# Row maxima placed by VectorE's load: one in diagonal pairs of steps, up to three in the others, 14 to 26 steps ahead of their scores

## What is computed

```python
latent_kv = x @ w_kv_down
kv = latent_kv @ w_kv_up
k, v = (kv[..., :HD], kv[..., HD:])
q = (x @ w_q).reshape(Bx, Tx, N_HEAD, HEAD_SIZE)
att = jnp.einsum('bqhd,bkhd->bhqk', q, k) * scale
att = jnp.where(causal, att, -jnp.inf)
att = jax.nn.softmax(att, axis=-1)
y = jnp.einsum('bhqk,bkhd->bqhd', att, v)
y = y.reshape(Bx, Tx, HD)
return y @ w_out
```

## Time and profile before

| | us |
|---|---|
| median of 3 runs | 2247.56 |
| lowest, highest | 2245.97, 2248.89 |
| the profiled execution | 2246.04 |
| its span, first to last instruction | 2244.7 |
| of it the attention steps | 330 to 2147 |

### The profile page before, as it was taken

One profiled execution on the slowest core, in us unless ns is written; L12 is line 12 of the kernel. 1 busy time (PEld: TensorE's weight loads), 2 busy tenths in 40 slices (PEclk: granted clock), 3 DMA queues, 4 the chain that ended last, 5 costly groups with the idle time before them and its releaser, 6 DMA issues.

```text
span 2244.7 us, 35674 instructions
## 1 busy us (share of the span) xinstructions
PE 2060.4 (92%) x13104; PEld 1269.9 (57%) x13104; DVE 1331.9 (59%) x2713; ACT 1102.8 (49%) x2226; POOL 1426.5 (64%) x812
## 2 busy tenths in 40 slices
PE   5998669999999999999989999999999999999989
PEld 3666345555555555555555555555555555555556
DVE  5888446575656565656565656566656565656353
ACT  4775534444444444444454444444444444444575
POOL 0333305776777777777757677777777777777832
PEclk9999769999999999999999999999999999999999
DMA  3000000000000000000000000000000000000001
GB/s 108 1 1 1 10 7 6 10 18 10 18 11 18 11 18 11 18 11 18 10 18 11 13 11 19 9 22 6 19 9 23 11 18 11 18 11 11 25 24 57
DMA packets 25788, 37.03 MB, mean 16 GB/s; under 512 B 6544, under 2 KB 14864, under 8 KB 25616
## 3 DMA queue, kind: packets, MB, share of 16 engines
q1 hardware_dynamic: 25616, 34.76, 5.0%
HBM read 30.02 MB, written 4.46 MB: 15 GB/s over the span
## 4 chain that ended last, share of the span: by engine, by line
PE 65%; DVE 19%; ACT 6%; issue 5%; POOL 4%; DMA 0%; ACTq 0%; DVEq 0%; POOLq 0%
PE heads_out L796 18%; PE beside L615 14%; PE two_heads L755 8%; PE scores L778 4%; PE scores L784 4%; PE scores L782 4%; PE scores L780 4%; DVE part_max L985 4%; PE scores L615 2%; POOL acc L1276 2%; ACT prob L1194 2%; DVE stats L835 2%; PE beside L807 2%; PE beside L763 1%; PE two_heads L615 1%
## 5 line engine op out<-in xcount | busy, mean ns | idle before, releaser
L1276 POOL TENSOR_TENSOR acc<-acc,prob 128x1024 f32<-128x1024 f32 (+3 forms) x512 | 1017.1, 1987 | 228.5 <-ACT prob L1194 172.7
L1194 ACT ACTIVATE prob<-scores 128x512 f32<-128x512 f32 (+3 forms) x1280 | 579.4, 538 | 636.4 <-DVE scores L995 327.8
L985 DVE TENSOR_REDUCE part_max<-two_heads 128x2 f32<-128x1024 f32 x384 | 468.7, 1221 | 309.1 <-PE two_heads L755 308.8
L796 PE MATMUL heads_out<-prob,V 128*64 128x512 f32 (+3 forms) x2560 | 549.1, 550 | 0.0
L755 PE MATMUL two_heads<-k_hi,q_hi 64*128 64x512 f32 (+3 forms) x1280 | 278.9, 431 | 70.2 <-DVE part_max L982 36.5
L982 DVE CUSTOM_DVE_ANT_0 two_heads<-two_heads,mask 128x128 f32<-128x128 f32 (+3 forms) x512 | 241.8, 514 | 119.2 <-PE two_heads L755 119.1
L796 PEld LDWEIGHTS heads_out<-prob,V 128*64 128x64 f32 x2560 | 157.8, 138 | 232.1 <-issue 210.4
L755 PEld LDWEIGHTS two_heads<-k_hi,q_hi 64*128 64x128 f32 x1280 | 121.3, 186 | 239.3 <-issue 102.4
L778 PE MATMUL scores<-q_hi,k_hi 64*128 64x512 f32 (+3 forms) x1280 | 236.9, 364 | 1.0 <-ACT neg_max L1181 0.8
L784 PE MATMUL scores<-neg_max,sel 64*128 64x512 f32 (+3 forms) x1280 | 236.9, 363 | 0.0
L782 PE MATMUL scores<-q_lo,k_hi 64*128 64x512 f32 (+3 forms) x1280 | 236.3, 363 | 0.0
(11 more groups left out here) (298 smaller groups left out, 3011.4 us busy)
## 6 DMA issues: line engine op xcount, KB each, us to landing
rden<-rden_rows SPq DMA_DIRECT2D x128, 128.0 KB, 2.9
wP_raw<-wPair SPq DMA_DIRECT2D x16, 384.0 KB, 3.2
X<-u SPq DMA_DIRECT2D x8, 512.0 KB, 8.7
out<-X SPq DMA_DIRECT2D x8, 512.0 KB, 2.9
den<-den_rows SPq DMA_DIRECT2D x64, 4.0 KB
rden_rows<-inverse SPq DMA_DIRECT2D x64, 4.0 KB, 1.4
wA_sb<-wA SPq DMA_DIRECT2D x1, 768.0 KB, 6.8
wFa<-wF SPq DMA_DIRECT2D x1, 768.0 KB, 7.7
```

Source lines behind the costliest of these rows:

```text
L796: made = pe.matmul(heads_out[head(h), x0:], V[(idx - j + c) % NVS][:, tt, head(h)], prob[step % NPROB][:, h, x0:], start=t == 0, stop=t == ...
L985: made = ve.reduce_max(part_max[:, t, :, c:c + 1], two_heads[:, :, 0:width], AX.X)
L1194: ac.activation(prob[step % NPROB][:, h, x0:], bank(task, h)[:, x0:], ACT.Exp).then_inc(empty(task, h)[0], 1)
L1276: po.tensor_tensor(total[:, :, x0:], total[:, :, x0:], new[:, :, x0:], ALU.add).then_inc(acc_ok, 1)
```

## The change

The lead stays 20 in the middle, but may swing by 6. A pair of steps is `diagonal` if one of its two steps is. In such a pair one maximum is placed, behind the scores, as long as the maxima are less than 26 steps ahead; in other pairs up to three, under the same limit; below 14 ahead up to three anywhere. The maximum ahead of the scores is left out in diagonal pairs, and wherever the last thing TensorE was given in the pair before is a maximum (`adjacent`); it then comes behind the scores, the filler or the weighings. `filler()` now says whether it placed something. `fillers()` is as before and reads `LEAD`, 20.

```diff
--- before.py
+++ after.py
@@ -29,7 +29,7 @@
 NPROB = 4
 NQ = 4
 NKS, NVS = 7, 6
-LEAD = 20
+LEAD, SWING = 20, 6
 NDEN, QUAD = 8, 32
 DVE_OUT = 62
 MIX = [(1, 0), (1, 1), (0, 0), (0, 1)]
@@ -351,9 +351,11 @@
 
         def filler(latest):
             open_ = sorted((x for x in fillers if x[0] <= s and x[2] not in self.done), key=lambda x: x[1])
-            if open_ and open_[0][1] <= latest:
-                fillers.remove(open_[0])
-                self.need(*open_[0][2])
+            if not open_ or open_[0][1] > latest:
+                return False
+            fillers.remove(open_[0])
+            self.need(*open_[0][2])
+            return True
 
         def output(idx):
 
@@ -379,7 +381,7 @@
         self.need("key", 1)
         self.need("query", 1)
         self.need("turn_max", 0)
-        self.in_steps = True
+        self.in_steps, adjacent = True, False
         for s in range(0, len(steps) + 2, 2):
             for load in sorted(x for x in loads if x[0] <= s):
                 loads.remove(load)
@@ -387,8 +389,10 @@
             for b in [STATS_BEFORE[UNITS[i]] for i in range(NU) if s == self.start[i] and UNITS[i] in STATS_BEFORE]:
                 side += self.mixer_stats(b, 2 if b else 3, NT)
             urgent = max([self.start[i] + TPB * (UNITS[i][2] + 1) for i in range(NU) if self.start[i] <= s + 4])
-            goal = min(len(maxima), max(urgent, min(s + 2 + LEAD, at + 3)))
-            if at < goal:
+            diagonal = any(t >= TPB * UNITS[idx][2] for idx, t in steps[s:s + 2])
+            ahead_of = max(min(s + 2 + LEAD + SWING, at + (1 if diagonal else 3)), min(s + 2 + LEAD - SWING, at + 3))
+            goal = min(len(maxima), max(urgent, ahead_of))
+            if at < goal and not diagonal and not adjacent:
                 maximum()
             due("invert")
             for step in steps[s:s + 2]:
@@ -406,12 +410,13 @@
                 if t == TPB * (UNITS[idx][2] + 1) - 1:
                     self.need("take_out", idx)
                     output(idx)
-            if at < goal:
+            adjacent = at < goal
+            if adjacent:
                 maximum()
             due("two_parts")
             due("scale_out")
-            if not due("denominators"):
-                filler(s + 8)
+            if due("denominators") or filler(s + 8):
+                adjacent = False
             if side:
                 self.add_all(side.pop(0))
             self.add_all(ahead.get(s - len(steps), []))
```

## The result

The changed kernel takes 2400.5 us (median of 4 runs, 2398.2 to 2413.2) against 2248.2 for the kernel before in the same session: 1.069 times as long, interval 1.067 to 1.072. The loss is 152 us where 87 were forecast, and 2400.5 is outside the range of 2280 to 2390.

What follows compares the result with a forecast made beforehand. TensorE was taken as the bound. Query waits of 99 us plus 58 us for maxima close together, less a 70 us gain, made +87 us: 2335 us, own range 2295 to 2375, widened to 2280 to 2390.

Steps and rivals of the forecast that it cites:

- The query's chain: Maxima directly behind their own query matmuls wait for `q_hi`, then `q_lo`: 53 new cases, 99 us lost.
- the price of `wP_lo`: Both halves, 1.06 us each on VectorE, between first and second maximum of three: 12 times 1.84 us, 22 us.
- the closeness: Maxima close to each other without long work between make TensorE wait: 58 us together, bounds 30 to 95.
- the 6 us of `turn_max`: Transposition needing bank 7 while VectorE's X add is behind a masked maximum: 16 times 0.4 us, 6 us.
- the clock: Rival: 5% of the attention steps' time, 91 us, falls to 1.2 GHz, losing 45 us: 2380 us; chance 0.07.
- The gain: Removed waits: 60 us of maxima, mostly behind diagonals' short scores, and 10 us of denominators for `k_lo`; 70 us.
- VectorE's busy time: Sign in the profile after: VectorE's busy time, like ScalarE's and GpSimd's, is the same within 1%.
- TensorE busy 87 to 88% of the steps: Sign in the profile after: TensorE is busy 87 to 88% of a longer stretch of attention steps.
- backlog: Rival: VectorE's work bunches in pairs with three maxima, 0.5 us at some 130 waits: +65, 2400 us; chance 0.09.
- only the queries: Rival: VectorE is always fast enough between maxima, so the 58 us falls away: 2277 us; chance 0.06.
- faster: Rival: the query's wait only replaces waits TensorE has anyway, leaving 58 less 70: 2235 us; chance 0.05.
- diagonals still wait: Rival: the change doesn't do what it says and diagonals still wait: +60, 2395 us; chance 0.03.

Runs made afterwards that it cites:

- e1_hold: Changed kernel, but queries or keys needed by the next eight maxima replace the filler, and no maximum stands directly behind its own query: 2297.9 us, 1.024.
- e2_forced: Kernel before, with queries from unit 3 on no longer fillers, so each is built directly ahead of its first maximum: 2328.3 us, 1.037.
- e5_hold_wlo_gpsimd: Changed kernel with no maximum directly behind its own query and the `wP_lo` subtractions moved from VectorE to GpSimd: 2232.1 us, 0.994.
- e6_spaced: Kernel before, lead 20, maxima behind scores and weighings, the latter left out ahead of a diagonal's end, made up behind a query or value: 2199.3 us, 0.980.
- e4_wlo_one_input: Changed kernel with the two-input `wP_lo` subtraction replaced by a one-input product of `wP_raw` with zero, same place: 2345.5 us (one run).
- e10_wlo_apart: Changed kernel with the two `wP_lo` halves in different pairs again, one ahead of `k_lo`, one behind the next maximum's reduction: 2347.5 us, 1.044.
- e3_wlo_gpsimd: Changed kernel with the `wP_lo` subtractions issued by GpSimd in place of VectorE: 2344.2 us, 1.043.

## Why the prediction was wrong, step by step

**The direction and the main term were right.** The query's chain was put at 1.57, 2.08 and 2.19 us in 26, 14 and 13 cases, 99 us. Its waits came to 82 us of idle time and 7 at `den_rows`. Taking it out gave 103 us (e1_hold); that this is so near 99 is luck, since 18 us of clock are in it, which the term didn't have, and 12 us of new waits work against them. Adding it to the order of before cost 95 us of waits and 82 of time (e2_forced). In the profile after, the case behind a full pair and the one behind the first pair of a diagonal read:

```profile
624.38 0.50 PE L760 MATMUL two_heads<-k_hi,q_hi 64*128 64x512 f32 x2 [1.50 <-DVE q_lo L973]
```

```profile
689.25 0.49 PE L760 MATMUL two_heads<-k_hi,q_hi 64*128 64x512 f32 x2 [1.66 <-DVE q_lo L973]
```

The mask holds the chain up less than I had it (1.66 us idle where 2.08 start to start were put, against 1.50 and 1.57 behind a full pair), and behind denominators the wait is divided: 1.50 for `q_lo` and 0.48 at the query's first matmul for `den_rows`, the 6.6 us of the last row of the waits; 1.98 in all against 2.19.

**The step that failed is the price of `wP_lo`.** I took 1.06 us for each half, the mean of the earlier trace rows, and 22 us for the 12 places. A group's mean is no price when the durations differ by four times: before, they ran from 0.415 to 1.704 us. It was the mean of four free ones and 28 that were held for the rest of one sum each, mostly 0.83 and 1.42. The change puts both halves behind each other into a stretch where GpSimd has 0.17 us between two sums, and so adds a whole sum. The chain from first to third maximum that I wrote as 5.77 us has 4.14 in place of 2.12, which is 2.0 more and 3.4 idle in place of the 1.84. That is 41 us of idle time and 56 to 66 us of time with what it does to the clock, where the sum had 22. It alone carries the closeness, 58 us, to the upper end of its bounds of 30 to 95: with the other waits of that kind in the trace (11.3 us at denominators, where I had 12; 9.5 at projections, where I had 10; 6.7 at keys, where I had 8; 6.8 behind the weighings of a short diagonal, where I had nothing) the idle time is 75 us, 90 to 100 with the price of `wP_lo` in full. The small terms were near. Of the 6 us of `turn_max` the list of waits shows nothing.

**The second failed step is the clock: the sum had nothing for it, and the rival with a chance of 0.07 came true.** I had 45 us if 91 us of the steps fell to 1.2 GHz; 90 us more did, worth some 40. Counted by kind and not by place, it is the larger half of the 65 us that the forecast lacked. My reason against it, that the waits are single ones among dense matmuls, is right as a picture and wrong as an argument: one wait of 3.4 us was followed by 3 to 4 us at 1.2 GHz. The Trainium skill's rule ("TensorE: Matmul & The Clock Gate", Part 1), that the clock is throttled unless TensorE's activity releases it, pointed this way, and I gave it too little. The total agrees with it (97 us more idle time, 90 us more at 1.2 GHz), e2_forced does not (89 us more idle time, 19 us less at 1.2 GHz). Part of this is in the amounts above and must not be added to them. The split by time, from the pairs of runs that differ in one thing, is

| | us | from |
|---|---|---|
| query waits | +103 | changed less e1_hold |
| `wP_lo`, with the query waits gone | +66 | e1_hold less e5_hold_wlo_gpsimd |
| all the rest of the change | -15 | e5_hold_wlo_gpsimd less before in its session (2247.5) |
| sum | +154 | measured 152 in the first session |

**The gain was overrated.** The waits behind short scores did go: behind the scores of 128 columns one of 0.6 us is left of 61 with 43.8 us. But the rest of the change, in which they stand as -70 and the other closeness as +36, was to give -34 us and gave -15. The 12 us of new waits that e1_hold itself makes are in this figure; without them it would be about -27, and the query waits about +115. One reason may be that idle time ahead of a matmul isn't all time that can be had back, though no run shows that for this order: e6_spaced has 2.9 us less of it in 40 steps than before (1.0 against 3.9) and is 1.8 us shorter (108.1 against 109.9). I had counted each at its idle time plus 0.1. The other way it doesn't hold: the changed kernel's 121.7 us are 11.8 more than 109.9, with 8.6 us more idle time and 3.4 us of low clock.

**VectorE's busy time** was to stay within 1%; it rose by 49 us, 3.7%. That line of the test pointed at the cause, since nothing was added to VectorE: the 32 instructions of `wP_lo` last 24 us longer in all (58.2 against 33.9). The rest is no work: all 2713 durations together grew by only 26 us, so the records overlap less. The sign "TensorE busy 87 to 88% of the steps" was no test: by my own sum it would be 1724 of 1904 us, 91%, and 1782.6 of 1973 is 90%. The other rivals, backlog, "only the queries", faster and "diagonals still wait", are out: the waits have their few places, and e5_hold_wlo_gpsimd is 168 us under the changed kernel. The backlog's 2400 us is the measured number by chance: it wanted 0.5 us in each of some 130 waits, and the price sits in 12 waits of 3.4 us and in the clock.

**Which wait brings the clock down?** In the changed order both kinds do. From 330 us to the end of the steps its trace has 33 stretches at 1.2 GHz. Nineteen of them, 82 us, begin within 4 us of the start of a query wait, of which there are 53; eleven, 38 us, within 5 us of the start of one of the 12 long waits. One behind a query wait:

```profile
612.00:622.00 10.00, 9.64 (x63) 6.16 (x60) 5.51 (x18) 4.19 (x9) 5.15 (x4) 1.00 0.01 2
622.00:632.00 10.00, 8.50 (x41) 4.18 (x39) 4.70 (x7) 2.26 (x6) 5.65 (x3) 0.83 0.10 27
632.00:642.00 10.00, 10.00 (x78) 6.30 (x78) 4.73 (x13) 6.00 (x15) 7.45 (x5) 1.00 0.01 2
```

Here a query wait of 1.5 us at 622.9 to 624.4 is followed by low clock. With the long waits gone or short and the query waits kept, low is 62 to 99 us (e4_wlo_one_input, e10_wlo_apart, e3_wlo_gpsimd), with the query waits gone and the long ones kept 91 (e1_hold), with both gone 32. So each kind brings some when the other is gone, and the query waits do so only in the changed order.

**What stays open** is why. In e2_forced none of the 59 query waits shorter than 2.7 us has low clock behind it, in the changed kernel 19 of 53 have, with the same 1.5 to 1.7 us. The length of the wait alone doesn't decide it, and no run separates what does.

## What to carry to other kernels

Before an instruction is moved, look at its durations one by one, not at the group's mean, and at what GpSimd does in the new place: a VectorE instruction of 0.4 us lasted 2.6 there. When work is pulled forward, give what it depends on the same head start, or the chain behind its producer opens in the bound engine's list, and spread the work of a second engine by giving each piece a long neighbour, not by a budget for each pair of steps: the even order won 2% where the uneven one lost 7%.

## What was unexpected of the hardware

- A 128x256 subtraction on VectorE took 0.42 us when no GpSimd instruction was running at its start, and otherwise ended 0.28 us behind that instruction, up to 2.59 us after its own start; two in a row took 4.14. `k_lo`, whose first input is a PSUM bank, kept its 0.68 us in the same stretch. The one-input form took 0.28 us free and up to 1.76 held, ending 0.15 us behind the sum.
- Behind one gap of 3.4 us among dense matmuls the granted clock of the next 4 us was 0.57. Gaps of 1.5 to 1.7 us had low clock behind them 19 times of 53 in one order, and not once in 58 in another.
- GpSimd did the same subtraction in 0.74 us, 32 times within 0.02.
